# A decoder layer on one core: three pairs of scan states summed on GpSimd, with another opening order, another share for ScalarE, another order in the DMA queue and in the tail before attention

## The reference

```python
xz = x @ in_proj_w.T;  u, z = split(xz)                    # 512 channels each
u = silu(causal_dwconv(u, conv_w, conv_b))                 # 4 taps
x_dbl = u @ x_proj_w.T;  dt, Bm, Cm = x_dbl[:16], x_dbl[16:32], x_dbl[32:48]
delta = softplus(dt @ dt_proj_w.T + dt_proj_b)
for t in time:                                             # h starts at zero
    h = exp(delta[t] * A) * h + (delta[t] * u[t]) * Bm[t]  # per channel and state
    y[t] = sum over the 16 states of h * Cm[t]
y = (y + u * D) * silu(z);  mamba = y @ out_proj_w.T
h1 = rmsnorm(mamba + x_normed);  x = x + rmsnorm(gelu(h1 @ w1) @ w2 + h1)
x = x + cross_attention(layernorm(x), context)
x = x + soft_moe(layernorm(x))
```

## Time and profile before

| | us |
|---|---|
| median of 3 runs | 1408.26 |
| lowest, highest | 1404.2, 1411.13 |
| profiled execution, its own time | 1410.29 |
| its span | 1408.5 |
| its parts: opening, scan loop, tail to attention, attention, experts | 48.8, 587.0, 71.6, 439.6, 261.5 |
| busy in the span: PE, ACT, DVE, POOL | 1272.4, 942.6, 749.1, 400.0 |

### The profile page before, as it was taken

One profiled execution on the slowest core, in us unless ns is written; L12 is line 12 of the kernel. 1 busy time (PEld: TensorE's weight loads), 2 busy tenths in 40 slices (PEclk: granted clock), 3 DMA queues, 4 the chain that ended last, 5 costly groups with the idle time before them and its releaser, 6 DMA issues.

```text
span 1408.5 us, 14664 instructions
## 1 busy us (share of the span) xinstructions
PE 1272.4 (90%) x5502; PEld 622.8 (44%) x5502; DVE 749.1 (53%) x840; ACT 942.6 (67%) x1340; POOL 400.0 (28%) x312
## 2 busy tenths in 40 slices
PE   5669997888988897899789999999999999999999
PEld 2234443434443363355522223223223235588988
DVE  4799989999999999984340000000000138560011
ACT  3867645677647854653399999999999975752300
POOL 1567765566646665750000000000000010000000
PEclk9789989899999998999999999999999999999999
DMA  5433585333323433459260000000000000202601
GB/s 163 152 119 120 174 234 199 110 122 120 120 90 128 136 129 110 149 183 238 70 181 1 1 1 1 1 1 1 1 0 1 1 0 30 78 13 103 286 16 45
DMA packets 43015, 127.73 MB, mean 91 GB/s; under 512 B 6103, under 2 KB 21399, under 8 KB 39544
## 3 DMA queue, kind: packets, MB, share of 16 engines
q1 hardware_dynamic: 42940, 126.75, 28.1%
HBM read 109.64 MB, written 17.09 MB: 90 GB/s over the span
## 4 chain that ended last, share of the span: by engine, by line
PE 57%; DVE 19%; ACT 16%; issue 6%; DMA 1%; POOL 0%; DVEq 0%; SPq 0%; ACTq 0%; POOLq 0%
PE ps L2070 11%; PE ps L2058 10%; DVE ps L1200 9%; ACT arena L1032 7%; PE ps L1857 5%; DVE arena L1211 4%; PE ps L2217 4%; PE ps L2260 4%; PE ps L2141 4%; PE ps L1918 3%; PE ps L1636 3%; ACT ps L806 2%; PE ps L1903 2%; PE ps L2235 2%; PE ps L2248 2%
## 5 line engine op out<-in xcount | busy, mean ns | idle before, releaser
L1032 ACT ACTIVATE arena<-ps,bound 128x1024 f32<-128x1024 f32 (+1 forms) x416 | 425.4, 1120 | 13.8 <-PE ps L2058 5.5
L625 POOL TENSOR_TENSOR arena<-arena 128x1024 f32<-128x1024 f32 x128 | 302.0, 2359 | 222.4 <-DVE arena L1211 168.9
L1200 DVE TENSOR_TENSOR_SCAN ps<-ps,arena 128x1024 f32<-128x1024 f32 x128 | 300.6, 2348 | 13.0 <-ACT ps L806 8.2
L1857 PE MATMUL ps<-arena,ident 128*128 128x512 f32 x512 | 241.7, 618 | 5.1 <-DVE arena L1211 5.1
L2058 PE MATMUL ps<-arena 97*128 97x512 bf16 (+1 forms) x832 | 214.0, 384 | 19.1 <-ACT arena L1032 13.7
L2070 PE MATMUL ps<-arena 128*32 128x512 f32 (+1 forms) x1664 | 207.3, 600 | 0.5 <-ACT arena L1032 0.5
L806 ACT ACTIVATE ps<-arena 128x512 f32<-128x512 f32 x256 | 166.2, 682 | 52.7 <-DVE arena L1211 48.8
L612 POOL TENSOR_TENSOR rstd<-ve,mhalf 128x4 f32<-128x4 f32 (+3 forms) x23 | 25.6, 1113 | 543.1 <-DVE ve L1496 467.0
L1523 DVE COPY arena<-ps 128x512 f32<-128x512 f32 x16 | 11.1, 691 | 288.7 <-PE ps L2070 288.7
L1211 DVE TENSOR_TENSOR arena<-ps,arena 128x1024 f32<-128x1024 f32 x128 | 155.8, 1217 | 10.6 <-DMA arena<-bc_scratch 4.7
L1857 PEld LDWEIGHTS ps<-arena,ident 128*128 128x128 f32 x512 | 99.9, 199 | 131.6 <-issue 120.8
(11 more groups left out here) (194 smaller groups left out, 1370.5 us busy)
## 6 DMA issues: line engine op xcount, KB each, us to landing
arena<-bc_scratch SPq DMA_DIRECT2D x128, 512.0 KB, 4.4
arena<-in_mw SPq DMA_DIRECT2D x16, 1024.0 KB, 9.0
qx_scratch<-arena SPq DMA_DIRECT2D x48, 128.0 KB, 3.1
arena<-qx_scratch SPq DMA_DIRECT2D x4, 1536.0 KB
arena<-kx_scratch SPq DMA_DIRECT2D x1, 4803.0 KB
kx_scratch<-arena SPq DMA_DIRECT2D x36, 128.0 KB, 4.4
arena<-vx_scratch SPq DMA_DIRECT2D x1, 3328.0 KB
vx_scratch<-arena SPq DMA_DIRECT2D x6, 512.0 KB, 2.9
```

What stands on the lines that cost most here:

```text
L625: pool.tensor_tensor(dbu[:, w % DR], du[:, DP * p:DP * p + DP], over(bg[:, w // BG % 2, n % BG], DP), ALU.mult).then_inc(S["dbu_ready"], 1)
L1032: act.activation(flat(prob[v % 3][0:n, 2 * h:2 * h + 2]), ps[0:n, 2 * (r % 3):2 * (r % 3) + 2, :].rearrange("p a b -> p (a b)"), ACT.Exp, ...
L1200: dve.tensor_tensor_scan(decay_banks(w), decay_banks(w), flat(dbu[:, w % DR]), carry[:, DP * p, n:n + 1], ALU.mult, ALU.add).then_inc(S["s ...
L1857: last = mm(bank(x), ident[:, :], state(2 * j + s)[:, x], start=False, stop=(j % HP == HP - 1 and (j in SUMMED or s == 1)))
```

## The change

1. **Pairs.** SUMMED = [57, 59, 61]: in the last chunk's second half GpSimd adds the two states of these pairs (`add_pair`, after the `scan_input` four steps later), and TensorE adds two matmuls instead of four, waiting for `pair_ready`.
2. **Opening.** VectorE starts with the layer norm and does the constants later; TensorE runs 18 matmuls on constants first (WARMING); the gates 0 and 1 of chunk 0 go to PSUM banks 2 and 3 right behind the channels; VectorE takes the Relu from ScalarE; ScalarE runs two dummy Exp that only load a table; VectorE itself makes the first product `dbu[0]` (`first_input`). In chunk 0, where the handed state is zero, the handed product, its decay and the 32 small adds on GpSimd are gone.
3. **ScalarE's share.** `step_rounded` leaves VectorE: ScalarE writes 1 + e (Identity with bias) behind `step_exp`, and VectorE's `step_rest` takes both subtractions. The sum is regrouped, so that only `step_size` needs the logarithm. `step_log` goes one step later (two before a new chunk). The layer norm of chunks 1 to 3 (`normed_input`, four instructions each) goes to ScalarE, VectorE keeps a 128 x 4 product (`input_shift`).
4. **Queue.** The value stores of chunk 0 and the weight loads go one or two pairs of steps later, and the loads no longer stand behind a wait for the key stores just issued.
5. **Tail.** The query squares of chunk 2 go to a buffer of their own and behind the first turn of the last chunk; TensorE takes both halves' projections before the lengths.

```diff
-SUMMED = []
+SUMMED = [57, 59, 61]
+WARMING = 18
+PREPARED = 3 + DB
...
+        squares = Stack(h1_at).take(DK, C)
...
             def load_ffn():
-                sp.wait_ge(S["vx_out"], 16 * len(VPAIRS))
                 sp.wait_ge(S["kx_out"], 16 * KSENT * len(KCOLS))
                 sp.wait_ge(S["row_out"], 16 * (NC + 1))
-                sp.dma_start(wout, wout_d).then_inc(S["w_out"], 16)
...
-                if q in (14, 15, 16):
-                    store_values(2 * q - 28)
-                    store_values(2 * q - 27)
+                if q in (15, 16, 17):
+                    store_values(2 * q - 30)
+                    store_values(2 * q - 29)
...
                 if q == 20:
+                    load_wout()
+                if q == 21:
                     store_keys(3, 2)
+                if q == 22:
                     load_ffn()
...
+                if c == 0:
+                    product.then_inc(S["dbu_ready"], 2)
+                else:
+                    product.then_inc(S["dbu_ready"], 1)
+                    pool.wait_ge(S["dbu_ready"], 2 * w - 1)
+                    pool.tensor_tensor(dbu[:, w % DR, 1, 0:1], dbu[:, w % DR, 1, 0:1], handed[:, p, n:n + 1],
+                                       ALU.add).then_inc(S["dbu_ready"], 1)
...
-                    scan_input(w)
+                    if w:
+                        scan_input(w)
...
                 act.activation(flat(sp_exp), flat(sp_exp), ACT.Exp, scale=-1.0).then_inc(S["sp_act"], 1)
+                act.wait_ge(S["sp_act"], softplus_steps(h) + 3)
+                act.activation(flat(sp_cor), flat(sp_exp), ACT.Identity, bias=1.0).then_inc(S["sp_act"], 1)
...
+            def normed_input(c):
+                act.wait_ge(S["shift_ready"], c)
+                for i in range(CT):
+                    act.activation(a0[:, c % 3, i], xt[:, c * CT + i, :], ACT.Identity, bias=crec[:, i:i + 1],
+                                   scale=rstd[:, i:i + 1]).then_inc(S["a0_ready"], 1)
...
                     if i == 5 + late:
                         step_exp(c, 1)
+                    if i == 6 + late:
                         step_log(c, 1)
-                    if i == 6 + late and more:
+                    if i == (6 if c == 1 else 7) and more:
                         turned_input(c + 1)
...
                     if i == 23 and more:
                         step_exp(c + 1, 0)
+                    if i == (25 if c else 24) and more:
                         step_log(c + 1, 0)
...
+                    if i == 5 and c == 0:
+                        normed_input(1)
+                    if i == 22 and c + 2 < NC:
+                        normed_input(c + 2)
...
+            def first_input():
+                dve.wait_ge(b_in[0], 16)
+                dve.wait_ge(S["du_ready"], 1)
+                dve.tensor_tensor(dbu[:, 0], du[:, 0:DP], over(bg[:, 0, 0], DP), ALU.mult).then_inc(S["prep_dve"], 1)
...
-                if i == 6 + late:
-                    step_rounded(c, 1)
...
-                        normed_input(c + 2)
+                        input_shift(c + 2)
...
+            for n in range(WARMING):
+                mm(bank(5)[:, 0:P], ones[:, :], ident[:, :], start=True, stop=True)
             turn_input(0)
...
-            pe.wait_ge(S["q_act"], q_count(2, "qsq"))
-            head_lengths(ps[0:NH, 1, :], xat[2])
             turn_half(0)
+            pe.wait_ge(S["q_act"], q_count(2, "qf"))
             project_half(0)
             turn_half(1)
+            project_half(1)
+            pe.wait_ge(S["q_act"], q_count(NC - 1, "qsq"))
+            head_lengths(ps[0:NH, 1, :], squares)
             lengths_half(0)
-            project_half(1)
             lengths_half(1)
```

192 lines of the change are left out of this document (108 added, 84 removed).

## The result

The changed kernel takes 1397.83 us (median of five, 1397.0 to 1398.8) against 1408.26: a ratio of 0.9917 (95% interval 0.9901 to 0.9933). It is faster, by 10.4 us in the medians and by 12.6 in the spans of the two profiled executions (1408.5 and 1395.9), where the prediction had 28.8. The direction was right; 16.2 us of the span's gain are missing.

A forecast was written before the change was run, and what follows sets the result against it. VectorE was taken as the scan loop's bound, TensorE as mostly the tail's. Opening 11.2, loop 16.2, pairs -1.4 and tail 2.8 sum to 28.8 us off the median 1408.3, giving 1379.5 us; range 1371 to 1394.

The forecast's parts named there:

- Opening: Start to first scan: four savings of 2.3, 2.1, 3.1 and 3.8 us, taken as 11.2; ends 5.5 to 12.
- stats, pace and x_proj terms: Opening: layer norm first 2.3 us, turn and first channel at full clock 2.1, x_proj sooner and faster 3.1.
- the collision: Opening: VectorE's first product might wait for GpSimd's product for step 1, scan 2.3 us later; taken as 0.
- Chunk 0, steps 0 to 20: Scan loop: normalizations, rounding and small products off VectorE, less a new ScalarE wait of 1.4 us; gain 5.5.
- Step 21 to chunk 1, step 2: Chunk change: savings and new ScalarE waits vanish behind gapless TensorE; only faster matmuls at its start gain 1.2 us.
- Rest of the loop: Rest of chunk 1 gains 5.0 us, chunk 2 3.8, chunk 3 to step 16 0.7.
- VectorE's waits for ScalarE grow beyond 10 us: Scan loop: one of the signs that the prediction named as proving it wrong.
- Pairs: Last half chunk: 57 and 59 save 3.5 us, pair 61 idles TensorE and slows its matmuls; 1.4 us lost in sum.
- Tail: After the scans: both projections first and lengths back to back gain 2.8 us; ends 1 and 3.5.
- Attention: Attention and experts: not touched, gain 0.
- Rival 1: Scan loop: TensorE and ScalarE set the pace, loop gives 6 us instead of 16.2, total 1389.7; chance 0.17.
- rival 2: Opening: clock does not rise or GpSimd wins the product, 5.5 us instead of 11.2, total 1385.2; chance 0.12.

The follow-up runs named there:

- changed_again: The changed kernel itself run once more, unaltered, on one chip as yardstick: 1397.72 us (1396.0 to 1399.8, six executions).
- lengths_first: Changed kernel with ScalarE's copy of the key lengths of block 2 one step earlier, ahead of the logarithm: 1391.67 us (0.9886).
- filled_five: Changed kernel with five zero-adding matmuls on all 128 rows in TensorE's hole before the value projections, copy still late: 1392.74 us (six executions).
- share_back: Changed kernel with part 3 undone: rounding and layer norm on VectorE again, logarithm behind the exponential in the same step: 1395.94 us (0.9914).
- two_pairs: both_mended without summed pair 61 (SUMMED = [57, 59]): 1387.76 us (0.985).
- norm_back: Changed kernel with the layer norm of chunk 2 given back to VectorE at chunk 0, step 20: 1396.2 us (0.9904).
- both_mended: Changed kernel with lengths_first's earlier copy, GpSimd's product for step 1 held behind VectorE's first product, and 20 warming matmuls: 1387.56 us (0.9865).
- filled_full: Changed kernel with four zero-adding matmuls on all 128 rows in TensorE's hole before the value projections: 1392.01 us (0.9877).
- filled_gap: Changed kernel with three zero-adding matmuls on 16 rows in TensorE's hole before the value projections: 1398.14 us (0.9939).

## Why the prediction was wrong, point by point

- **Opening: right but for the choice between two ends.** 11.2 predicted, 8.85 measured. The stats, pace and x_proj terms are right within 0.1 us together. The term that failed here is "VectorE needs no signal from another engine, so I take 0" for the collision: GpSimd's product was released by the same signal and was 0.07 us ahead; the 2.3 us named for it were 2.1.
- **Chunk 0, steps 0 to 20: 5.5 predicted, 2.5 measured.** Two steps were mis-sized. The normalization at step 4 gave its 2.9 us, but that at step 20 only 1.13, since the small product that stayed on VectorE (0.15 us alone) took 2.29 beside GpSimd's product; another such meeting made an addition of step 8 3.19 us long (2.57 before). And the new waits were 3.2 us, not 1.4: 1.59 for TensorE at step 6 (its clock stood at 0.50 from 50.2 to 63.9 us), 1.09 and 0.55 for ScalarE. In *changed_again* step 20 met nothing and gave 2.2 us, so part of this is chance.
- **Step 21 to chunk 1, step 2: the step that failed.** The prediction said that all new ScalarE waits vanish behind a TensorE that runs without a gap over 56 us. It costed ScalarE against VectorE only and took TensorE's missing gap for a property of the stretch. It was one only while ScalarE kept up. Instead of 1.5 to 1.9 us, VectorE's new waits for ScalarE were 10.0 (1.48, 4.63, 2.70 and 1.22), and they did not vanish. In the old kernel the copy of the key lengths (L855) ended at 169.89, and the projections that need it followed at 171.50, straight behind the pair before them:

```profile
167.97 3.70 PE L1857 MATMUL ps<-arena,ident 128*128 128x512 f32 x8
171.50 1.03 PE L1661 MATMUL ps<-arena 96*128 96x256 f32 x4
...
169.69 0.20 ACT L855 ACTIVATE arena<-ps 128x64 f32<-128x64 f32 x1
```

  That slack of 1.6 us was to be read. In the changed kernel the pair (155.08) comes 12.9 us earlier and the copy (161.18) 8.5 us earlier; the difference, less the slack, is 2.8 us, which is the idle time of 2.65. It became a halved clock, and 1.2 us of gain became 6.15 of loss. *lengths_first* and *filled_five* show that the late copy and the clock behind it are the cause, *share_back* that they come from ScalarE's new share. What makes the clock fall is known only as far as the count above: *two_pairs* lost it without idle time.
- **Rest of the loop: 9.5 predicted, 6.1 measured.** Wait for loads and waits in chunk 2, step 8 went as said. What was short are waits for ScalarE behind its new instructions: 0.36, 0.43 and 0.66 us in chunk 1, steps 26 to 28, 1.28 at chunk 2, step 7, and 0.64 for TensorE at chunk 2, step 2. The condition "VectorE's waits for ScalarE grow beyond 10 us" was met: 13.7 us before the scans and 4.6 before the heads, against 10.0.
- **Pairs: right in kind.** The scans came 1.4 us earlier (2 predicted), TensorE idled 2.33 us before pair 61 (4.2 predicted) because pair 60 had taken 5.38 us instead of 3.7, and no slow matmuls followed; 0.14 instead of -1.4. That was luck: of the eleven traces with an idle time of 2.3 us there, nine kept the clock and two lost it (*lengths_first*, *norm_back*), with -2.3 and -2.4 us for the stretch. With the faster loop of *both_mended* it came as the prediction had it: 4.02 us of idle time and half pace behind it.
- **Tail: right**, 2.72 for 2.8.
- **Attention: "not touched" was wrong in time.** 1.5 us were lost there again. The work is the same, and over all 17 traces this part grows, nearly in order, with the time until the clock is back (701.1 us after 4.1, 703.0 after 9.3), so I put it down to the clock.
- **Rivals.** Rival 1 (TensorE and ScalarE set the pace in the loop, 6 us instead of 16.2) had the mechanism nearly right and was still too mild, and rival 2's collision came true with it. Each was priced alone, at 1389.7 and 1385.2; together they leave 12.9 us of the 28.8, which is about the result, though by other shares (the loop gave 2.4 us, not 6, the opening 8.85, not 5.5). The range left out that they could come together.

## What to carry to other kernels

Before work is moved to an engine with idle time, list every copy that another engine takes from it and read each slack from the trace; with TensorE a missed slack of a microsecond or two can cost several times its length through the clock (here 2.65 us of idle time went with some 8 us of lead). Put short hand-overs ahead of long work and table loads in the same step: here one copy moved by a step gave more than all of ScalarE's new share. And when two engines are released by one signal and may share a path, order them by a wait instead of taking the cheap end.

## What the runs showed of the hardware

- TensorE's clock fell to its lower level after quite short idle times at the change of chunks: 0.86 us (*filled_full*), 1.31 (*filled_gap*), 1.84, 2.65, 3.49, 4.08 us; after 0.64 us in *share_back* it didn't. In *two_pairs* it fell with no idle time to speak of, where the stretch holds projections on 96 rows and single-row matmuls, and in *both_mended*, the same code there, it did not. It stayed low some 10 to 17 us.
- Three filling matmuls on 16 rows with 1.31 us of idle time behind them, and four on 128 rows with 0.86 us, didn't keep it up; five on 128 rows with none did in the profiled execution and, by the times, brought 5 us. The number of rows and the idle time are not told apart.
- The same idle time of 2.3 us before pair 61 left the clock at full in nine traces and halved it in two.
- The same idle time of 5.1 to 5.7 us before the scores is followed by 4.1 to 9.3 us at half clock, from trace to trace; the part behind it takes 701.1 to 703.0 us with it.
- 18 warming matmuls that ended 1.14 and 1.16 us before the work began protected the transposes (1.74 us) but not the channels after them (12.23 us instead of 10.54); with 1.05 us and less the channels kept their pace.
- A product of 4 columns on VectorE took 0.15 us alone and 2.29 beside GpSimd's product.
